# Four more left tiles of a symmetric attention map multiplied as two halves

## The reference

```python
g_x = einsum('oc,bchw->bohw', g_w, x) + g_b      # 128 x 4096 per image
f = einsum('bnc,bcm->bnm', theta, phi)           # theta, phi both are x: f = x^T x, 4096 x 4096, symmetric
attn = softmax(f, axis=-1)
y = einsum('bnm,bmc->bnc', attn, g_x)
wy = einsum('oc,bchw->bohw', W_w, y) + W_b       # then batch norm over all images
return wy + x
```

## Time and profile before

| what | us |
|---|---|
| median of 3 runs | 2054.38 |
| profiled execution, as a run | 2054.48 |
| its span | 2052.8 |
| PE busy | 2006.7 |
| VectorE busy | 1545.2 |
| ScalarE busy | 1157.2 |
| GpSimd busy | 888.3 |

### The profile page before, as it was taken

How to read it: one execution, slowest core, us unless ns; L and a number is a source line. 1 busy time by engine, 2 the same in 40 slices (tenths; PEclk the granted TensorE clock), 3 DMA queues, 4 the chain that set the end, 5 groups by cost and what they waited for, 6 DMA issues and landing times.

```text
span 2052.8 us, 28691 instructions
## 1 busy us (share of the span) xinstructions
PE 2006.7 (98%) x9428; PEld 1466.5 (71%) x9428; DVE 1545.2 (75%) x3116; ACT 1157.2 (56%) x2391; POOL 888.3 (43%) x688
## 2 busy tenths in 40 slices
PE   5999999999999999999999999999999999999999
PEld 4787777766688777776678777776668877777444
DVE  6777777877777777797777777787777777777777
ACT  4345556666444546667554555666644454666657
POOL 3011224779602124678821122567960202467740
PEclk9999999999999999999999999999999999999999
DMA  3222333556511332565622233465651132245998
GB/s 138 106 90 79 121 108 125 190 180 196 167 68 67 129 103 93 173 209 158 215 85 85 77 108 119 128 191 167 196 181 67 67 123 94 92 143 187 354 336 328
DMA packets 107507, 299.94 MB, mean 146 GB/s; under 512 B 11488, under 2 KB 11872, under 8 KB 93536
## 3 DMA queue, kind: packets, MB, share of 16 engines
q1 hardware_dynamic: 107360, 298.11, 43.0%
HBM read 157.55 MB, written 140.51 MB: 145 GB/s over the span
## 4 chain that ended last, share of the span: by engine, by line
PE 86%; ACT 4%; DVE 4%; issue 3%; POOL 3%; DMA 1%; SPq 0%; DVEq 0%; ACTq 0%; POOLq 0%
PE bank L1412 15%; PE bank L1333 12%; PE bank L1335 12%; PE bank L1334 12%; PE bank L1384 9%; PE bank L1423 5%; PE bank L1416 5%; PE bank L1417 5%; PE bank L1576 3%; PE bank L1487 2%; ACT ring L905 1%; DVE bank L1155 1%; ACT phi L946 1%; PE bank L1340 1%; PE bank L1368 1%
## 5 line engine op out<-in xcount | busy, mean ns | idle before, releaser
L946 ACT CAST phi<-bank 128x512 fp32r<-128x512 f32 x480 | 280.8, 585 | 594.9 <-PE bank L1384 594.4
L1109 DVE TENSOR_SCALAR_CACHE_REDUCE ring<-bank 128x512 f32<-128x512 f32 x560 | 386.1, 689 | 242.2 <-PE bank L1335 190.7
L1333 PE MATMUL bank<-xh 128*128 128x512 f32 (+3 forms) x1152 | 508.7, 442 | 4.0 <-POOL xl L785 3.6
L1140 DVE TENSOR_TENSOR plo<-bank,phi 128x512 fp32r<-128x512 f32 x480 | 329.6, 687 | 141.3 <-ACT phi L946 111.2
L1335 PE MATMUL bank<-xh,xl 128*128 128x512 f32 (+3 forms) x1152 | 435.2, 378 | 0.0
L1334 PE MATMUL bank<-xl,xh 128*128 128x512 f32 (+3 forms) x1152 | 433.0, 376 | 0.0
L905 ACT ACTIVATE ring<-ring,nmax 128x512 f32<-128x512 f32 x464 | 334.5, 722 | 1.0
L1384 PEld LDWEIGHTS bank<-ident,ring 128*128 128x128 f32 x1856 | 223.4, 140 | 120.2 <-issue 61.3
L825 POOL TENSOR_TENSOR fy_d<-fy_d,maxrow 128x512 f32<-128x512 f32 x173 | 224.3, 1300 | 183.7 <-DMA fy_d<-spill 183.7
L825 POOL TENSOR_TENSOR fy_c<-fy_c,maxrow 128x512 f32<-128x512 f32 x193 | 249.6, 1297 | 107.3 <-DMA fy_c<-spill 107.2
L1384 PE MATMUL bank<-ident,ring 128*128 128x128 f32 x1856 | 279.7, 273 | 10.2 <-DVE plo L1140 8.0
(11 more groups left out here) (165 smaller groups left out, 2933.2 us busy)
## 6 DMA issues: line engine op xcount, KB each, us to landing
spill<-ring SPq DMA_DIRECT2D x108, 1024.0 KB, 4.4
fy_c<-spill SPq DMA_DIRECT2D x200, 256.0 KB, 4.1
fy_d<-spill SPq DMA_DIRECT2D x180, 256.0 KB, 4.1
ring<-x_dram SPq DMA_DIRECT2D x42, 512.0 KB, 5.8
lbuf<-spill SPq DMA_DIRECT2D x68, 256.0 KB, 5.0
yd<-yn SPq DMA_DIRECT2D x24, 256.0 KB, 3.4
out_dram<-ring SPq DMA_DIRECT2D x10, 512.0 KB, 3.4
fx_a<-x_dram SPq DMA_DIRECT2D x8, 512.0 KB, 7.2
```

The source lines that it names most:

```text
L1109: last = nc.vector.tensor_scalar(slot_tile(u, t), src, 1.0, None, ALU.mult, ALU.max, accum_out=rowm[:, t, c:c + 1])
L1140: nc.vector.tensor_tensor(plo[:, n % LOS, :], whole(p), phi[:, HI_BUF[n], :].bitcast(F32), ALU.subtract).then_inc(lo_made, 1)
L1333: nc.tensor.matmul(dst, xh[:, k, rows], xh[:, k, cols], start=(k == 0), stop=False)
```

## The change

One condition of `SELF` is widened. Before, blocks 3 and 4 had their left tiles of the chunk before their own, and of their own, split; now it is all chunks from 2 on. For block 3 that is the same list. Block 4 gets the four tiles of chunk 2 added.

```diff
-SELF = [p for p in LEFT if (tile(p)[0] in (3, 4) and tile(p)[1] >= tile(p)[0] - 1) or tile(p)[:2] == (5, 5)]
+SELF = [p for p in LEFT if (tile(p)[0] in (3, 4) and tile(p)[1] >= 2) or tile(p)[:2] == (5, 5)]
 SELF_AT = {p: min(w for w, q in enumerate(LEFT) if q > p + 3) for p in SELF}
 SPLIT = [p for p in range(TILES) if not tile(p)[3] or p in SELF]
```

## The result

The changed kernel takes 2059.14 us (median of 15 runs, 2056.61 to 2062.87), the kernel before in the same comparison 2054.88 us (15 runs, 2052.21 to 2058.34). The ratio is 1.0023 with an interval of 1.0016 to 1.003: 4.3 us slower (3.3 to 6.2), against a forecast of 2058.2, which was 3.7 us above the profiled execution it started from. The profiled execution of the changed kernel took 2059.14 us too, its span is 2057.4 us, and the granted clock of TensorE is 1.0 as before, its upper level of 2.4 GHz.

The account below looks back on a forecast made before the run. PE bounds the kernel (98% busy), but GpSimd's list decides at the changed tiles. Net of 0.7 us saved per image, three images lose 0.9 and one 1.0: +3.7 on 2054.48 gives 2058.2 us, range 2053.0 to 2062.0.

Parts of the forecast that it names:

- PE saves 0.17 us per tile: PE, block 4's four added split tiles: three products take 0.69 us against 0.85 or 0.86, 2.7 us in 4 images.
- ScalarE's copies, cost 0: ScalarE, high halves of 146, 148, 149, 151: four copies of about 0.5 us, none of them what PE waits for.
- GpSimd at tile 149, the step that decides: GpSimd's low half of 149 comes late, so PE's third product waits 1.8 us in image 1, 1.3 in image 3.
- 0.1 us at tile 151: PE, tile 151's third product: wanted at 885.59, started at 885.71 because GpSimd's low half is ready only at 885.66.
- Net of a block: Block 4 on PE, savings and waits together: 0.9 us later in three images and 1.0 in the last.
- Behind it, cost 0: GpSimd's work queued after the added low halves, subtractions 156 and 157 and low 154: just fits, cost 0.
- The seam, cost 0: Between two images, high half 0 waits for tile 253, not 254; ScalarE is busy until the same moment, so nothing.
- rival C: Loads of tiles 149 and 151 slip, each us costing PE one in images 0 to 2; 2061.8 at 1.2 us; chance 0.21.
- B, the cover holds: GpSimd's low halves of 148, 149 and 151 come before PE wants them, leaving 2.7 us saved: 2051.8; chance 0.14.
- D, the two cancel: Waits at tiles 149 and 151 equal the 0.7 us saved per image, PE reaching 149 later: about 2054.5; chance 0.13.

Follow-up runs that it names:

- the first experiment: Kernel before with only tiles 146 and 151 of chunk 2 split as well, loads as in the changed kernel: 2058.24 against 2054.93 us, 1.0017.

## Why the prediction was right, and where not

**PE saves 0.17 us per tile: right.** At the start of step 149 two of the four have been multiplied, and the changed kernel is 0.32 us ahead in image 1 and 0.34 in image 3, where 0.34 was due. In block 2 it is 0.14 per tile; I did not trace where the rest of it stays. The estimate from the 4 passes that the Trainium skill ("FP8 and Floating Point Precision", TensorE Precision Notes) gives for true float32, a quarter of 0.86 per tile, would put it 0.43 ahead at that point, which the trace does not show.

**ScalarE's copies, cost 0: the times right, the margin not seen.** ScalarE in image 1:

```profile
879.85 0.62 ACT L946 CAST phi<-lbuf 128x512 fp32r<-128x512 f32 x1 [0.89 <-PE bank L1423]
...
881.09 0.61 ACT L946 CAST phi<-fy_c 128x512 fp32r<-128x512 f32 x1
...
884.54 0.61 ACT L946 CAST phi<-fy_d 128x512 fp32r<-128x512 f32 x1
```

Less 1.59, the copies of 148, 149 and 151 end at 878.88, 880.11 and 883.56; the forecast said 878.8, 880.0 and 883.5. No product waits for a copy. But the step asked only whether the copies are in time, not what they push back. With GpSimd's passes shortened they cost 0.3 to 0.7 us per image through the right exponentials (block 4 with the shorter passes, without and with the exponentials ahead). "Cost 0" was true because GpSimd's wait covered it.

**GpSimd at tile 149, the step that decides: right.** Subtract 151 began at 879.51 - 1.59 = 877.92 (forecast 878.12), and the three passes after it ran back to back to the end of low 149, as in the list. PE reaches tile 149 when forecast (882.56 - 1.59 = 880.97 against 880.96), and its wait is 1.56 us (forecast 1.8; the 0.2 are the subtraction's). That the subtraction of 151 began near the forecast time has another reason than the one given: the prediction let it wait for its own load, but it stands without a gap behind low 146, and the run of passes begins when the load of 149 is there (877.00, [0.68 <-DMA]). In image 3 the forecast was 1.3, and the product is 1863.18 - (1861.52 + 0.23) = 1.43 us late:

```profile
1861.52 0.39 PE L1417 MATMUL bank<-phi,gl 128*128 128x512 f32 x1
1863.18 0.51 PE L1423 MATMUL bank<-plo,gh 128*128 128x512 f32 x1 [1.27 <-POOL plo L798]
```

```profile
1859.34 1.30 POOL L798 TENSOR_TENSOR plo<-lbuf,phi 128x512 fp32r<-128x512 f32 x1 [1.31 <-ACT phi L946]
```

Low 148 starts there within 0.1 us of the forecast, but the profile names the copy of high half 148 as what it waited for last, and not the buffer of `plo` that the prediction named. By the profile that copy and the product of tile 146, which frees the buffer, end within 0.03 us of each other, so both hold it.

That low 149 is late because three passes of GpSimd don't fit into PE's way from 146 to 149 is also what the shorter passes show: with 0.76 in place of 1.29 that product of image 1 starts 0.3 us late (882.53, due at 881.99 + 0.23) in place of 1.56.

**0.1 us at tile 151: right.** Its third product starts at 887.07, where 886.73 + 0.23 = 886.96 was due; in the other images it is late by 0.15, 0.14 and 0.03. That is too short to show in the list of waits.

**Net of a block: 0.9, 0.9, 0.9, 1.0 forecast; 0.93, 0.66, 0.97, 1.09 measured.** Sum 3.65 against 3.7. That the sum agrees so closely is partly luck: image 1 is off by 0.24, and the second trace of the same kernel gives 4.10.

**Behind it, cost 0: right.** The shift at step 160 is that of step 152 within 0.04 us in all four images, and no wait for L798 stands in tiles 152 to 157.

**The seam, cost 0: wrong by 0.3 us in one seam of three.** "ScalarE is busy until the same moment" holds in two seams; in the one from image 1 to 2, [0.16 <-issue] stands before high half 0 in the kernel before, and PE is 0.29 ahead with tile 253's buffer. I looked at the number for 144 tiles only. With 142 the same rotation costs 1 us per seam, and my expectation for the first experiment, which took it for nothing, failed by 3 us.

**The loads (rival C): a small part, and not where I put it.** In the changed kernel's first trace no load makes tile 146 late. Over the eight traces of kernels that split it, its third product is late in some images: 0.1 to 1.8 us in 12 of the 24 images 0 to 2, never in image 3, 0.3 us per image on average. I had rival C at tile 149; the place is 146, because low 146 stands behind the subtraction of 149 and that behind its load. The moved loads cost the head start too: from the load of 149 on, GpSimd works through the list, and the wait at 149 is 1.56 to 1.68 us in images 0 to 2 against 1.43 in image 3, where the loads are early. So earlier loads might give back 0.1 to 0.25 us per image, an estimate from these waits; I did not run the changed kernel with the loads of the kernel before.

**Rivals B and D.** B, the cover holds (2051.8), would have needed low 149 ready by 881.4; it was ready at 884.53 - 1.59 = 882.94. Faster GpSimd passes alone don't bring it about, and with ScalarE's order besides block 4 comes out at -0.11 in place of -2.7; whether VectorE's part would bring the rest is not shown. D, the two cancel, would have needed PE to reach 149 half a microsecond later, and it was there to 0.01 us.

The rest between 2058.2 and the measured 2059.14 is smaller than the scatter of start and end from one execution to the next.

## What to carry to other kernels

When work is moved to an engine with idle time, add up its list between the moment at which the first input is there and the moment at which the result is wanted; the busy share of the span says nothing on that. Then take the late engine away in thought and ask which one is next: here three engines stood within about half a microsecond of each other, and no single repair that I tried brought the gain. And when a count changes that runs through a ring of buffers, look at where the ring wraps, however far from the edit that is.

## What the runs showed of the hardware

One thing was not expected. A load of the same size from the same queue position took different times to its use from one trace to the next: that of tile 149 in image 2, queued behind one x load, was issued at 1359.62 and its subtraction began at 1367.53 in one kernel, 7.9 us, and was issued at 1360.51 and there by 1366.49, at most 6.0 us, in the changed one:

```profile
1359.62 1.56 SPq L687 DMA_DIRECT2D fy_c<-spill  x1
```

```profile
1360.51 0.47 SPq L687 DMA_DIRECT2D fy_c<-spill  x1
```

The issue itself took 1.56 us in the one and 0.47 in the other, but that is not the reason by itself: in image 1 of the changed kernel the issue took 1.36 us, and the subtraction began 5.7 us after its start. What made the load slower in the one is open. GpSimd's pass was steadier: nine in ten take 1.26 to 1.31 us for 512 columns, and all take 0.72 to 0.77 for 256, so about 0.2 us of it (an estimate from the two) doesn't shrink with the columns.
